# Attention scores of two heads in the two 64-row halves of the array, in fp32r parts, with one maximum operation for both heads

## The reference

```
x = x + 0.5 * ffn(layernorm(x));  x = x + attn(layernorm(x));  x = x + 0.5 * ffn(layernorm(x))

# attn: q, k, v = h @ W.T + b, split in 16 heads of 16
scores = einsum('bqhd,bkhd->bhqk', q, k) / sqrt(16)
attn = softmax(where(causal, scores, lowest))
o = einsum('bhqk,bkhd->bqhd', attn, v);  return o @ Wo.T + bo

# ffn: 4-bit weights, dequantised; 2048 wide
out = (gelu_tanh(x @ Wg.T) * (x @ Wu.T)) @ Wd.T
```

## Time and profile before

| | us |
|---|---|
| median of 3 runs | 1139.37 |
| range of them | 1133.9 to 1139.43 |
| the profiled execution | 1138.86 |
| its span | 1137.2 |

### The profile page before, as it was taken

The page is one execution under the profiler, slowest core; times in us unless marked ns, Lnnn a source line. Parts: engine busy times, 40 slices in busy tenths (PEclk is TensorE's granted clock), DMA queues, the critical chain, the costliest instruction groups (busy, mean ns, idle before and its releaser), DMA issues. The chain is left out here.

```text
span 1137.2 us, 17563 instructions
## 1 busy us (share of the span) xinstructions
PE 1082.1 (95%) x6448; PEld 710.4 (62%) x6448; DVE 694.4 (61%) x1606; ACT 582.9 (51%) x1112; POOL 112.1 (10%) x409
## 2 busy tenths in 40 slices
PE   4999999998998999999999999999989999999998
PEld 3888888886875433333333333333358888888887
DVE  5986545447465577887888888888333434344333
ACT  5764443432334645656677776777752433324222
POOL 1000000000001226231111111111100000000000
PEclk9999999998998889999999999999999999999999
DMA  6001030250030911322022202200000000000000
GB/s 191 2 21 28 10 120 1 48 149 1 13 119 1 229 34 39 81 52 52 1 53 53 50 3 53 52 2 1 1 1 1 1 4 16 1 19 1 19 1 19
DMA packets 75223, 43.81 MB, mean 39 GB/s; under 512 B 47161, under 2 KB 68993, under 8 KB 75137
## 3 DMA queue, kind: packets, MB, share of 16 engines
q1 hardware_dynamic: 75137, 42.68, 15.2%
HBM read 25.63 MB, written 16.78 MB: 37 GB/s over the span
## 5 line engine op out<-in xcount | busy, mean ns | idle before, releaser
L1010 ACT ACTIVATE attn_prob<-psum 128x512 f32<-128x512 f32 (+3 forms) x640 | 301.5, 540 | 145.4 <-PE psum L694 141.6
L1153 DVE TENSOR_REDUCE attn_part_max<-psum 128x1 f32<-128x512 f32 x384 | 244.0, 685 | 56.8 <-PE psum L709 54.9
L606 PE MATMUL psum<-ffn_xt,all_w_hi 128*128 128x512 f32 x512 | 166.1, 406 | 0.0
L753 PE MATMUL psum<-attn_prob,attn_vals 128*32 128x512 f32 (+3 forms) x1280 | 160.5, 556 | 4.1 <-ACT attn_prob L1010 2.9
L1349 PE MATMUL psum<-ffn_xt,all_w_hi 128*128 128x512 f32 x512 | 160.5, 395 | 2.4 <-DVE ffn_xt L1486 2.4
L1156 DVE CUSTOM_DVE_ANT_0 attn_junk<-psum,attn_mask 128x128 bf16<-128x128 f32 (+3 forms) x256 | 117.3, 486 | 27.9 <-PE psum L709 27.3
L1496 DVE TENSOR_TENSOR ffn_act_out<-ffn_act_out,psum 128x512 f32<-128x512 f32 x64 | 44.1, 689 | 108.4 <-ACT ffn_act_out L1419 108.4
L621 PE MATMUL psum<-all_w_hi,ffn_inner 128*128 128x256 f32 x512 | 105.0, 288 | 0.1
L1349 PEld LDWEIGHTS psum<-ffn_xt,all_w_hi 128*128 128x128 f32 x512 | 92.9, 190 | 18.9 <-DVE ffn_xt L1486 2.6
L606 PEld LDWEIGHTS psum<-ffn_xt,all_w_hi 128*128 128x128 f32 x512 | 92.7, 192 | 16.5 <-issue 0.3
L1419 ACT ACTIVATE ffn_act_out<-psum 128x512 f32<-128x512 f32 x64 | 38.4, 599 | 125.7 <-PE psum L1349 124.9
(11 more groups left out here) (138 smaller groups left out, 1529.9 us busy)
## 6 DMA issues: line engine op xcount, KB each, us to landing
qk_rows<-qkv_parts SPq DMA_DIRECT2D x16, 384.0 KB, 2.6
qk_rows<-qkv_parts SPq DMA_DIRECT2D x16, 256.0 KB, 3.0
attn_q_early<-qk_rows SPq DMA_DIRECT2D x8, 384.0 KB, 4.4
attn_q_late<-qk_rows SPq DMA_DIRECT2D x8, 384.0 KB, 3.9
attn_k_mid<-qk_rows SPq DMA_DIRECT2D x3, 768.0 KB, 7.1
attn_k_late<-qk_rows SPq DMA_DIRECT2D x3, 768.0 KB, 6.9
all_x<-in_L_attn_h SPq DMA_DIRECT2D x4, 512.0 KB, 6.2
v_rows<-qkv_rows_v SPq DMA_DIRECT2D x16, 128.0 KB, 2.6
```

The source lines that it names most:

```text
L606: last = nc.tensor.matmul(psum[:, 2 * m + q % 2, :], w_part[a][:, 3 * g + m, pl, o:o + P], xt[:, b % 2, c, pl, :], start=(n == 0), stop=(n ...
L753: last = nc.tensor.matmul(psum[r:r + 32, O0, at:BT], vals[:, k0 * SUB + kb + k, 2 * hd:2 * hd + 32], prob[:, (4 * d + 2 * k + hd) % PRING, ...
L1010: nc.scalar.activation(prob[:, n % PRING, at:BT], psum[:, S0 + n % SBANKS, at:BT], ACT.Exp).then_inc(s["exp"], 1)
L1153: nc.vector.tensor_reduce(to, psum[:, bank, :], AX.X, ALU.max).then_inc(s["max_read"], 1)
```

## The change

q and k are now cut into two fp32r parts, and three products are summed: 3 x 16 = 48 rows a head (`KR`), with two rows for the maximum and two of -1, so 50 rows. Head 0 of a pair lies in partitions 0 to 63 and head 1 in 64 to 127, in one tile, which is fp32 and takes both heads by one DMA. A matmul of head 0 uses the upper 64 rows of the array and one of head 1 the lower. The scale of 1/4 is applied in the exponential.

```diff
-NPART = 3
-Q_PARTS = (0, 0, 0, 1, 1, 2)
-K_PARTS = (0, 1, 2, 0, 1, 0)
-KR = len(Q_PARTS) * HD
-MBANKS = 3
+NPART = 2
+KR = 3 * HD
...
+                def head(hd, n):
+                    return slice(HALF * hd, HALF * hd + n)
...
-                            nc.tensor.matmul(psum[:, S0 + n % SBANKS, at:BT], keys(k0 + c)[part, hd, 0, o * P:(o + 1) * P],
-                                             queries(b)[part, hd, g % 2 * BT + at:g % 2 * BT + BT], start=True, stop=True).then_inc(s["scored"], 1)
+                            nc.tensor.matmul(psum[:, single_bank("score", 4 * d + j), at:BT], keys(k0 + c)[part, o * P:(o + 1) * P],
+                                             queries(b)[part, g % 2 * BT + at:g % 2 * BT + BT], start=True, stop=True).then_inc(s["scored"], 1)
```

```diff
+                        def half(e, hd, place):
...
+                            if place == 0 and ("max", e) in pair_use:
+                                pair_free("max", e)
+                            bank, part = pair_bank("max", e), head(hd, KR)
...
+                            last = nc.tensor.matmul(psum[:, bank + hd, 0:cols], queries(b)[part, g % 2 * BT + i * P:g % 2 * BT + (i + 1) * P],
+                                                    keys(k0 + c)[part, 0:cols], start=True, stop=(c < qt), skip_group_check=True)
+                            if c < qt:
+                                last.then_inc(s["max_scored"], 1)
+                            elif place == 1:
+                                for a in range(2):
+                                    nc.tensor.matmul(psum[:, bank + a, cols - P:cols], identb[:, :], mask[:, :], start=False, stop=True,
+                                                     skip_group_check=True).then_inc(s["max_scored"], 1)
...
+                            dve.wait_ge(s["max_scored"], 2 * e + 2)
+                            nc.vector.tensor_reduce(part_max[:, g % 2, :, i, c], psum[:, bank:bank + 2, 0:cols], AX.X, ALU.max
+                                                    ).then_inc(s["max_read"], 1)
```

```diff
+            S0, O0, PAIRS = 3, 2, (0, 6)
+                return S0 + single_use[kind, n] % SBANKS if (kind, n) in single_use else 4
+                return PAIRS[pair_use[kind, n] % 2] if (kind, n) in pair_use else 4
...
-            EARLY_SLOTS = {1: 6, 2: 6, 3: 6, 4: 6, 11: 5, 12: 5, 13: 5, 14: 5, 15: 4}
+            EARLY_SLOTS = {1: 3, 2: 2, 3: 3, 4: 2, 11: 2, 12: 3, 13: 3, 14: 3, 15: 3}
```

```diff
-                            nc.scalar.activation(full[:, n % 2, :], psum[:, unit_bank(n), :], ACT.Identity,
...
-                            nc.scalar.activation(parts[:, n % 2, 0, :], full[:, n % 2, :], ACT.Copy).then_inc(s["part_1"], 1)
...
-                            nc.scalar.activation(parts[:, n % 2, 1, :], rest[:, n % 2, :], ACT.Copy).then_inc(s["part_2"], 1)
+                            nc.scalar.activation(parts[:, n % 2, 0, :], psum[:, unit_bank(n), :], ACT.Identity,
+                                                 bias=bias[:, kind, half:half + 1]).then_inc(s["hi"], 1)
...
+                            nc.vector.scalar_tensor_tensor(parts[:, n % 2, 1, :], psum[:, unit_bank(n), :], bias[:, kind, half:half + 1],
+                                                           as_f32(parts[:, n % 2, 0, :]), ALU.add, ALU.subtract).then_inc(s["lo"], 1)
...
-                            sp.dma_start(queries(b)[0:KR, :, :], qk_dram[0, 2 * p:2 * p + 2, :, qt * BT:cols].rearrange("h r t -> r h t")
+                            sp.dma_start(as_f32(queries(b)), qk_dram[0, p, :, qt * BT:cols]).then_inc(s[f"stack{b}"], 16)
```

356 lines of the change are left out of this document (163 added, 193 removed).

## The result

| kernel | median us | runs | ratio to before, 95% interval |
|---|---|---|---|
| before | 1138.9 | 1133.9 to 1139.43 | |
| changed | 1270.76 | 1268.14 to 1273.03 | 1.117 [1.113, 1.121] |

What follows compares the result with a forecast made beforehand. PE's own work was taken to fill attention's full steps, with the score-exponential-product chain deciding after the change. Terms -2 - 8 - 2 + 0 + 3 + 2 = -7 us gave 1132 us, range 1104 to 1166 (the case's own 1118 to 1146).

Steps and rivals of the forecast that it cites:

- Full step 2.76: Attention's main part: a full step takes 2.76 us between products, the middle of 2.70 to 2.82, against 2.84 before.
- 14 steps 39.0: Attention's main part: 14 steps take 39.0 us instead of 39.27, counted as -2 us over seven periods (-10 to +13).
- a mask before the product: Diagonal chunks' masks on PE directly before the product: 0.15 us each for four of them, 0.34 at most.
- the gather step: Attention steps with a gather: 3.2 us (3.0 to 3.4), as now, with DVE's 1.2 us read lying beside the gather.
- DVE -8 in steps 9 to 48: Attention steps 9 to 48: DVE's chunk work falls from 102.7 to 94 us, saving 8 us (-14 to +6).
- Last block of the projection -2: Stretch to 388 us: ACT loses eight operations, 2.5 + 2.5 us, counted as -2 us (0 to -5).
- Maxima in the last feed-forward block 0, to +5: Last feed-forward block: 1.3 us of matmuls between chunks against 1.2 of DVE, so 0 us (-2 to +5).
- End +3: The 12 steps behind the last chunk get only the weight loads, 12 x 0.24, so +3 us.
- Clock +2, to +10: Attention: one more fall of PE's clock to 1.2 GHz, +2 us (0 to +10).
- the sign of a wrong reason: Attention's main part: a clock below 0.97, or a time over 15 us from 273, would mean the forecast's reason is wrong.
- My second rival: PE's clock falls in ten more places, gather steps above all: +20 us on the forecast, 1150 us; chance 0.12.
- The rival without overlap: Scores and halves don't overlap, each mask costs 0.34 us: 14 steps take 43.7 us, in all 1189 us; chance 0.14.

Runs made afterwards that it cites:

- e9: Changed kernel with scores and halves of chunks over all 64 rows of their half instead of 50 and 48; 1228.50 us, ratio to before 1.080.
- e6: e1 with each DVE read of a chunk's maxima cut to 2 x 64 elements; 1185.91 us, ratio to before 1.042.
- e13: e9 with a separate maxima read for each head, freeing single banks instead of pairs; 1228.74 us, ratio to before 1.084.
- e12: Changed kernel writing one copy of a unit's parts to DRAM instead of three in the projection's last block; 1266.95 us, ratio to before 1.115.
- e15: Changed kernel, 50 and 48 rows kept, with each read of a chunk's maxima cut to 2 x 64 elements; 1204.52 us, no interval.
- e1: Changed kernel with every score and half of a chunk on all 128 array rows, so none overlap; 1246.77 us, ratio to before 1.097.
- e7: e1 without the two mask matmuls of a diagonal chunk; 1232.42 us, ratio to before 1.083.
- e11: Kernel before with scores and maxima contracting over 75 rows instead of 99 and 96; 1155.84 us, ratio to before 1.017.
- e5: Kernel before with scores and maxima contracting over 50 rows (maxima 48) instead of 99 and 96; 1484.83 us, ratio to before 1.305.
- e10: e9 with a step's third chunk moved behind the product of the step before on PE; 1230.28 us, ratio to before 1.082.

## Why the prediction was wrong, point by point

**Full step 2.76: right in kind, a little too long.** 2.67 us (660.22 to 662.89), just under the lower bound of 2.70. The last half's load is hidden, as at the lower bound.

**14 steps 39.0: near.** 39.58 us against 39.27 before. Ten full steps at 2.67 instead of 2.76 take 0.9 us off my sum, and this hides two terms that were too small: a mask before the product 0.22 us (taken: 0.15), and the gather step 3.53 us (taken: 3.2). I had laid DVE's read beside the gather; in the trace the gather itself waits for it:

```profile
675.24 1.05 PE L786 MATMUL psum<-attn_pick,attn_o_sb 128*128 128x34 f32 x8 [0.34 <-DVE attn_part_max L1150]
```

With e9's clock of 1.00 the main part is 277.73 us, +2.9 where I had -2, inside the bounds of -10 to +13.

**DVE -8 in steps 9 to 48: this step failed, in its overlap.** DVE's own times were right: DVE's groups by form in attention,

```profile
L1150 DVE TENSOR_REDUCE attn_part_max<-psum 128x2 f32<-128x1024 f32 x212 | 255.2, 1224 | 129.2 <-PE psum L721 101.9 <-PE psum L727 27.1
```

1.22 us as forecast. But I costed DVE by its busy time, in a stretch where it was not the bound. What counts is when the banks come free: PE and DVE took turns, 40 us by e6 with the clock mostly full, for which my sum had an upper bound of +6. Whether that is due to the pairs or just to the length of a read stays open (e13).

**Last block of the projection -2: wrong.** +14.4: 6.4 for the landing of the writes (e12), the rest open. I counted the removed ACT operations and not that `full` had stood between PE's bank and the DMAs.

**Maxima in the last feed-forward block 0, to +5: at the bound.** +4.6; with short reads the first product comes at 361.24 us instead of 365.53 (e15), so 4.3 of it is DVE's read in front of PE. I had set six feed-forward matmuls (1.3 us) against 1.2 us of read, and left no room for the masks and the wait of each.

**End +3: right but for the clock.** 31.34 us in e9, +2.5; 39.97 with the clock at 0.70.

**Clock +2, to +10: this is the step that failed most.** It cost some 70 us: 51 (estimate) in steps 9 to 48, 10.0 in the main part, 8.6 in the end. The clock of the main part, 0.96, is also below the 0.97 that I had named as the sign of a wrong reason. My second rival had the mechanism, the clock falling again and again, but priced it at ten short falls, 1150 us, where whole stretches ran at 1.2 GHz (product 8 to 20: 0.50 throughout). Three things were wrong in my reasoning. I read the earlier trace rows as a matter of PE's busy time and did not look at rows, of which there were 99 and would be 50. And I held against the rival that behind the last chunk PE had kept its clock with 1.7 of 2.4 us of work: that was at 99 rows, and at 50 the same stretch ran at 0.70. I took a stretch as evidence in which the change would alter the very thing that matters. And I priced clock and bank waits as if each stood alone, while the waits brought the clock down too (short reads alone: 0.55 to 0.78).

**The rival without overlap** gave 43.7 us for 14 steps and 31.8 for the end; e1, which is that kernel, has 43.98 and 31.57. The mix was another (masks 1.0 instead of 2.7 us; a gather step 4.10 us, read the same way, instead of 3.22), and its total of 1189 us fell short of 1246.77 by the reads, which no case of mine contained. That e6, which is e1 with short reads, comes to 1185.91 is luck in part: steps 0 to 8 took 12.9 us more than before, where the rival had nothing, and steps 9 to 48 6.6 more, where it had 16.

What stays open: why e15 stays at 1.2 GHz up to step 20 and not behind it; 8 us of steps 0 to 8; and whether pairs of banks or long reads make PE wait. The share of clock and ring in steps 9 to 48, which pull on each other, is an estimate by subtraction. Why the writes need longer to land than before was not tried.

## What to carry to other kernels

That a matmul over half the rows costs the same time does not make the smaller contraction free. In these kernels PE's clock went with the rows at work, so ask of every change that packs or shortens a contraction how many rows it leaves active, above all where PE has gaps, and fill them up with harmless rows if the layout has them (e9: -42 us for two slices). When fewer, larger operations take over from many small ones, ask how long each holds its buffers and who waits for them; their busy time, which fell here, does not tell. And price waits and clock together: here the clock rose from 0.55 to 0.78 by shorter waits alone (e15). And a stretch that has kept its clock proves nothing for a kernel with other rows in it.

## What the runs showed of the hardware that was not expected

- In the main part, where PE has next to no gaps, the granted clock was 1.00 with 99 and with 75 rows (before, e11), and with 50 rows 0.50 for all of 511.84 us in which PE was never idle (e5).
- Where PE has gaps, the same code lands at different clocks: e13 took 1210.73 us at a mean clock of 0.949 and 1228.63 at 0.928, and the end, the same code in both, took 31.34 us at 1.00 in e9 and 40.83 at 0.68 in e10.
- Extra full-array matmuls between two half-array ones lowered the clock with one a chunk (0.55 in the main part, from 0.96) and raised it with two (0.99).
- Matmuls in the two row halves started within 0.01 us of each other, their weight loads too, and each took as long as a matmul of e1, where all run one by one (0.50 us behind a wait, 0.40 else). A mask on the full array behind them and before the product made the step 0.22 us longer, against 0.12 where all matmuls have 128 rows (e1, e7).
